# Adding up sixteen scan states with accumulating transfers, and moving upper adjacency products from a middle pass into the scan

## The chip, the cores and the metric

The kernel runs on one core of one Trainium2 chip. The metric is the device time of one launch in microseconds (us), as the median of several runs.

## What is computed

Two layers over a graph of N = 8192 nodes with 128 features, each with a residual. Layer 0 is a graph convolution with a symmetrically normalised adjacency matrix. Layer 1 is a graph convolution with the plain matrix, a layer norm and a selective state-space block (Mamba) that scans over the 8192 nodes with 256 inner channels and 16 states:

```
h = relu(layernorm(x));  D = sum(adj, axis=1);  d = D ** -0.5
x = x + relu(((adj * d[:, None] * d[None, :]) @ h) @ W.T + b)
h = relu(layernorm(x))
g = layernorm(relu(adj @ h @ gcn_w + gcn_b)) * ln_g + ln_b
xz = g @ w_in;  u = silu(conv4(xz[:, :256]));  z = xz[:, 256:]
dt, B, C = from u @ w_xp;  dt = softplus(dt @ w_dt + b_dt);  A = -exp(A_log)
s[t] = exp(dt[t] * A) * s[t-1] + dt[t] * B[t] * u[t]        # 256 x 16 states
y[t] = sum over the 16 states of s[t] * C[t]
x = x + ((y + u * D_skip) * silu(z)) @ w_out
```

All arithmetic is float32. The matrix is 256 MB, does not fit on the core, and is read more than once.

## The kernel before

**Tiling.** The output nodes are cut into 8 strips of 1024 columns. A block is 256 source nodes by one strip: 1 MB in SBUF, two pieces of 128 x 1024. A product here is one 128x128 by 128x512 matrix product; a block needs 4 of them for each layer. A float32 product shows as two PE records, a product of split operands (float32r) as one.

**Pass A** reads the whole matrix, adds up the degrees on VectorE (line 550), and forms layer 0 for every block on or below the diagonal (line 731).

**The middle (pass B)** goes through the strips from 6 down to 0 and reads the blocks above the diagonal once more. For layer 0 they complete the strip; a strip of layer 0 then gives 1024 nodes of layer 1's input `h1`, which are just the source nodes that the next strips need. So layer 1's upper products are formed from the same loads. Strip 6 (`firsts`) does this in plain float32, 16 products for each layer. Strips 5 to 0 split every operand in a high and a low float32r part: ScalarE writes the high parts (`high_part`, lines 1021 and 1024), VectorE subtracts for the low parts (`low_part`, lines 572 and 577), and TensorE forms high x high, high x low and low x high (`split_product`, line 813). That is 6 matmuls per piece and layer. `adj_parts` has two buffers, so ScalarE may start piece r only when TensorE has finished piece r-2. VectorE also completes the strip before (`complete`, seven stages, one after each of the first seven pieces), and ScalarE normalises it after piece 7 (`layer1_input`). Strips 5, 4, 3, 2, 1, 0 have 16, 24, 32, 40, 48, 56 pieces.

**The scan stage (pass C)** runs over 16 chunks of 512 nodes. A chunk has 16 slots, one for each state; slot g of the whole stage is state g mod 16 of chunk g div 16. In slot g VectorE multiplies (line 653) and scans twice (line 664, once for each half of the channels); GpSimd multiplies the state by C (line 458); ScalarE forms the next decay (line 1099). TensorE broadcasts row B for the next slot (line 874), which it may do only when the scans of slot g-1 are done, because the PSUM banks are shared. The other steps of a chunk stand in fixed slots: `chunk_at(g, STAGE)` says in which. Counted within a chunk, the convolution and gate products (lines 928, 932) are in slots 4 to 7, line 940 in 10, `dt` in 12 and 13, `gcn` in 13, the output products (line 909) in 9, skip, gate and residual on VectorE in 4, 5 and 9. TensorE works ahead on the strips of layer 1 that lie after it: `products[g]` spreads the products of strips 1 to 7 evenly over slots -19 to 204, at the end of each slot (line 853). Strip 7 is whole before slot 205. Slots -19 to -1 have no scan yet.

**The sum over the states.** GpSimd adds the two states of a pair (line 462), in all but the last 3 chunks, and TensorE adds the pairs up in PSUM, by products with the identity (line 890): two for each added pair, four for each pair that was not added. The ring of state buffers, `hs`, has 8 entries; an entry comes free when its identity products are done:

```
                    if g >= HSB:

                        dve.wait_ge(nsum_done, (g - HSB) // 2 + 1)
```

Layer 1's upper sums of strips 0 to 6 go to DRAM in the middle (`move_layer1`) and come back in the scan stage, where VectorE adds them (line 640).

**Queues.** SP issues all loads of the matrix (line 393) and, in the scan stage, the rows of C (line 418), in slot order; a load of C waits for GpSimd's products two pairs back. ScalarE issues the small transfers. GpSimd issues none.

## Time and profile before

| | |
|---|---|
| median of 3 runs | 2683.72 us (2681.23 to 2686.16) |
| the profiled execution, its own time | 2687.66 us |
| its span | 2685.8 us, so 1.9 us lie around it |
| mean granted TensorE clock | 0.954 of full speed |
| busy in the span | PE 87%, DVE 78%, ACT 36%, POOL 35% |
| HBM traffic | 239 GB/s over the span |

The stages follow each other: pass A to 792 us, the middle to 1427 us, the slots before the first scan to 1508.65 us, the scan to the end. In the profile a row gives an engine, a line, an operation, output <- inputs, and the mean time of one in ns; "idle before" is how long the engine had nothing to do and who ended that. PE durations contain the pipeline's tail, so the spacing of matmuls in a dense run, not their duration, is what one costs.

### The profile page before, as it was taken

Reading aid. Unit: us, or ns where it says so; the run is one execution under the profiler, and the core shown is the slowest. Engines: PE = TensorE matmul, PEld = TensorE weight load, DVE = VectorE, ACT = ScalarE, POOL = GpSimd, SP = SyncE. Lnnn points to the kernel's source line nnn. Section 1 sums busy time; section 2 is a strip of 40 time slices with the busy share of each in tenths; the row PEclk is TensorE's granted clock in tenths of the full one; section 3 lists DMA queues with packets and bytes.
Section 4 is the critical chain, followed back from the end, with each engine's and each line's share of the span. In section 5 each row is a group of like instructions: output and inputs, shape, how many; then the busy total and the mean of one; then the engine's idle time right before and its main releaser. Section 6 shows DMA issues by size and latency. Waiting matters only on the chain.

```text
span 2685.8 us, 22298 instructions
## 1 busy us (share of the span) xinstructions
PE 2325.4 (87%) x7072; PEld 1314.6 (49%) x7072; DVE 2082.0 (78%) x2079; ACT 979.5 (36%) x1696; POOL 936.9 (35%) x409
## 2 busy tenths in 40 slices
PE   0347688999999999999999989999999989997776
PEld 0113344444447888888885444444444444443333
DVE  5888888886645666566652599999999899999997
ACT  0000000000004555555552455555545555555552
POOL 0000000000000000000000388777778788787554
PEclk9978789999999999999999999999999999998898
DMA  8999999898766555555547655555555555551121
GB/s 337 380 398 412 394 393 388 356 404 321 263 247 236 214 214 216 197 213 196 199 183 266 231 198 210 207 208 204 198 211 213 197 207 206 204 196 63 67 75 52
DMA packets 108325, 643.02 MB, mean 239 GB/s; under 512 B 14225, under 2 KB 15025, under 8 KB 42673
## 3 DMA queue, kind: packets, MB, share of 16 engines
q1 hardware_dynamic: 92160, 604.02, 59.3%
q10 hardware_dynamic: 16048, 37.57, 4.0%
q8 instruction: 58, 0.95, 0.1%
q14 instruction: 59, 0.48, 0.0%
HBM read 625.28 MB, written 16.25 MB: 239 GB/s over the span
## 4 chain that ended last, share of the span: by engine, by line
PE 57%; DVE 28%; issue 8%; ACT 3%; ACTq 1%; DMA 1%; DVEq 0%; POOL 0%; SPq 0%; POOLq 0%
PE ps L813 21%; PE ps L731 13%; DVE arena L550 11%; PE ps L853 10%; DVE arena L664 6%; DVE ps L653 6%; PE ps L890 4%; PE ps L928 4%; PE ps L753 2%; ACTq L958 1%; DMA diag_h<-adj 1%; PE ps L874 1%; PE ps L909 1%; DVE ring L664 1%; PE ps L932 1%
## 5 line engine op out<-in xcount | busy, mean ns | idle before, releaser
L813 PE MATMUL ps<-adj_parts,h_parts 128*128 128x512 f32 x2592 | 593.7, 391 | 2.5 <-ACT adj_parts L1024 2.2
L442 POOL TENSOR_TENSOR rstd<-base,minus_half 128x8 f32<-128x8 f32 (+1 forms) x40 | 84.7, 2118 | 1450.7 <-DVE base L490 877.9
L853 PE MATMUL ps<-ring,diag_h 128*128 128x512 f32 x1152 | 549.0, 611 | 0.3 <-DVE arena L640 0.2
L458 POOL TENSOR_TENSOR arena<-arena 128x1024 f32<-128x1024 f32 x192 | 458.5, 2394 | 251.1 <-ACT state L1091 251.1
L813 PEld LDWEIGHTS ps<-adj_parts,h_parts 128*128 128x128 f32 x2592 | 485.0, 188 | 108.6 <-ACT adj_parts L1024 4.7
L550 DVE TENSOR_TENSOR arena<-arena,ring 128x2048 f32<-128x2048 f32 x208 | 476.8, 2292 | 67.0 <-DMA ring<-adj 49.2
L731 PE MATMUL ps<-ring,arena 128*128 128x512 f32 x928 | 437.7, 633 | 62.4 <-DMA ring<-adj 62.4
L664 DVE TENSOR_TENSOR_SCAN arena<-arena,state,ps 128x512 f32<-128x512 f32 x384 | 470.6, 1267 | 26.1 <-DVE ps L653 1.0
L853 PEld LDWEIGHTS ps<-ring,diag_h 128*128 128x128 f32 x1152 | 223.8, 196 | 252.4 <-issue 249.3
L1099 ACT ACTIVATE arena<-arena,a_sb 128x512 f32<-128x512 f32 x512 | 338.3, 708 | 0.4
L577 DVE TENSOR_TENSOR adj_parts<-ring,adj_parts 128x1024 fp32r<-128x1024 f32 x216 | 264.0, 1224 | 94.3 <-ACT adj_parts L1024 83.5
L731 PEld LDWEIGHTS ps<-ring,arena 128*128 128x128 f32 x928 | 187.4, 204 | 305.5 <-issue 305.5
L653 DVE TENSOR_TENSOR ps<-arena,ps 128x1024 f32<-128x1024 f32 x256 | 311.3, 1216 | 22.1 <-PE ps L874 21.1
L874 PE MATMUL ps<-parts,pick 96*128 96x512 f32 x256 | 181.2, 708 | 101.2 <-DVE arena L664 87.8
L1024 ACT ACTIVATE adj_parts<-ring 128x1024 fp32r<-128x1024 f32 x216 | 226.7, 1052 | 112.9 <-PE ps L813 110.9
L965 ACT ACTIVATE arena<-arena,nmr,rstd 128x128 f32<-128x128 f32 x128 | 51.9, 482 | 497.4 <-DVE nmr L494 497.4
L890 PE MATMUL ps<-arena,ident 128*128 128x512 f32 x456 | 229.9, 637 | 0.0
L462 POOL TENSOR_TENSOR arena<-arena 128x1024 f32<-128x1024 f32 x78 | 183.7, 2356 | 6.1
L664 DVE TENSOR_TENSOR_SCAN ring<-arena,state,ps 128x512 f32<-128x512 f32 x128 | 156.9, 1267 | 24.9 <-ACT arena L1099 18.1
L753 PE MATMUL ps<-ones,arena 128*128 128x1 f32 x256 | 47.2, 319 | 142.1 <-DVE arena L550 142.1
L458 POOL TENSOR_TENSOR ring<-ring,arena 128x1024 f32<-128x1024 f32 x64 | 151.3, 2365 | 24.5 <-ACT state L1091 24.5
L874 PEld LDWEIGHTS ps<-parts,pick 96*128 96x128 f32 x256 | 50.1, 196 | 203.7 <-issue 203.7
(85 smaller groups left out, 1783.1 us busy)
## 6 DMA issues: line engine op xcount, KB each, us to landing
ring<-adj SPq DMA_DIRECT2D x480, 1024.0 KB, 6.5
arena<-c_scratch SPq DMA_DIRECT2D x128, 512.0 KB, 3.8
diag_h<-adj SPq DMA_DIRECT2D x32, 1024.0 KB, 12.2
arena<-x ACTq DMA_DIRECT2D x16, 512.0 KB, 4.7
x_scratch<-arena ACTq DMA_DIRECT2D x8, 512.0 KB, 3.0
arena<-x_scratch ACTq DMA_DIRECT2D x16, 256.0 KB, 4.3
out<-arena ACTq DMA_DIRECT2D x16, 256.0 KB, 3.0
lower_scratch<-arena ACTq DMA_DIRECT2D x7, 512.0 KB, 2.6
```

The costliest lines, as they stand in the source:

```text
L458: nc.gpsimd.tensor_tensor(buf, buf, c_row, ALU.mult).then_inc(mult_done, 1)
L550: nc.vector.tensor_tensor(rowacc, rowacc, v, ALU.add).then_inc(adds_done, 1)
L577: nc.vector.tensor_tensor(adj_parts[:, buf, 1, :], ring[:, slot_of[q], a * STRIP:(a + 1) * STRIP], adj_parts[:, buf, 0, :].bitcast(F32), A ...
L653: nc.vector.tensor_tensor(dbu_ps[g % 2], w[k % 2], b_ps[g % 2].unsqueeze(1).to_broadcast([P, HALVES, T]), ALU.mult)\
L664: nc.vector.tensor_tensor_scan(hs[g % HSB][:, h, :], da[g % 2][:, h, :], dbu_ps[g % 2][:, h, :], state[:, h, n:n + 1], ALU.mult, ALU.add). ...
L731: last = nc.tensor.matmul(acc[:, c, :], tile_of(h, JT * s + a), blk[:, a * STRIP + c * MM:a * STRIP + (c + 1) * MM], start=start and a == ...
L813: last = nc.tensor.matmul(acc[:, c, :], h_parts[:, blk % 2, layer, h_part, a * F:(a + 1) * F], adj_parts[:, buf, adj_part, c * MM:(c + 1) ...
L853: last = nc.tensor.matmul((acc_c if i else y_ps)[:, c, :], tile_of(h1, JT * s + a), blk[:, a * STRIP + c * MM:a * STRIP + (c + 1) * MM], s ...
L874: nc.tensor.matmul(b_ps[(g + 1) % 2], pick[:, nn:nn + 1].to_broadcast([KP, P]), pv[0:KP, :], start=True, stop=True).then_inc(b_ready, 1)
L890: last = nc.tensor.matmul(y_ps[:, h, :], ident[:, :], term[:, h, :], start=pair == 0 and j == 0, stop=pair == DS // 2 - 1 and j == len(ter ...
L1024: nc.scalar.activation(adj_parts[:, buf, 0, :], ring[:, slot_of[q], a * STRIP:(a + 1) * STRIP], ACT.Copy).then_inc(hi_ready, 1)
L1099: last = nc.scalar.activation(da[(g + 1) % 2][:, h, :], dt[k % 2][:, h, :], ACT.Exp, scale=a_sb[:, h, n:n + 1])
```

## The change

Two things. First, the sum over the states. GpSimd writes its products of states 0 and 1 into a new tile `y_pair`; the product pairs of states 2 to 13 are added to it by six transfers from SBUF to SBUF of 128 x 2048 floats (1 MB) each with `accum_op=ALU.add`, issued from GpSimd's queue. Each waits until the one before has landed (`y_added`). TensorE then takes the two halves of `y_pair` in slot 16 (slot 0 of the next chunk, four identity products), and the last pair, states 14 and 15, directly in slot 18 (four more). GpSimd's own additions are gone. `hs` has 6 entries in place of 8; entries of states 2 to 13 come free when their transfer has landed.

Second, strips 2 to 6 form layer 1's upper products in the scan stage, in plain float32, and no longer in the middle; their blocks are read again there, and their upper sums no longer go through DRAM. Strips 0 and 1 keep the old way.

```diff
-HSB = 8
+HSB = 6
+DEFERRED = 2
-NSUM = 6
+YSUM, LAST_PAIR = 16, 18
-SPARED = 3
...
-    rows_of = {i: list(range(BPS * (i + 1))) for i in range(NS)}
+    rows_of = {i: list(range(BPS * (i + 1) if i < DEFERRED else NB)) for i in range(NS)}
...
+        PAIRS = DS // 2
+
+        def added(G):
+
+            k, p = divmod(G, PAIRS)
+            return 16 * ((PAIRS - 2) * k + min(max(p - 1, 0), PAIRS - 2))
...
-                    nc.gpsimd.tensor_tensor(buf, buf, c_row, ALU.mult).then_inc(mult_done, 1)
-                    if g % 2 and g // 2 < PAIRS_ADDED:
+                    k, n = divmod(g, DS)
+                    if n == 0 and k:
+
+                        pool.wait_ge(nsum_done, 2 * k - 1)
+                    nc.gpsimd.tensor_tensor(y_sums[n] if n < 2 else buf, buf, c_row, ALU.mult)\
+                        .then_inc(mult_done, 1)
+                    if n % 2 and 2 < n < DS - 2:
+
                         pool.wait_ge(mult_done, g + 1)
-                        even = hs[(g - 1) % HSB]
-                        nc.gpsimd.tensor_tensor(even, even, buf, ALU.add).then_inc(pair_done, 1)
+                        pool.wait_ge(y_added, added(g // 2))
+                        pool.dma_start(y_pair, hs_pairs[g // 2 % (HSB // 2)], accum_op=ALU.add)\
+                            .then_inc(y_added, 16)
...
-                        dve.wait_ge(nsum_done, (g - HSB) // 2 + 1)
+                        k_old, n_old = divmod(g - HSB, DS)
+                        if n_old < 2:
+                            dve.wait_ge(mult_done, g - HSB + 1)
+                        elif n_old < DS - 2:
+                            dve.wait_ge(y_added, added((g - HSB) // 2 + 1))
+                        else:
+                            dve.wait_ge(nsum_done, 2 * (k_old + 1))
...
-            for layer, acc, h in ((0, acc0[NS % 2], h0), (1, acc1, h1)):
...
+            for s in firsts:
+                product(acc0[NS % 2], h0, s, arrived(load_at["B", NS - 2, s]), s == firsts[0], s == firsts[-1])\
+                    .then_inc(blocks_done, 1)
...
                     last = split_product(acc0[i % 2], r, a, 0, start, stop)
-                    if stop:
-                        last.then_inc(layer0_sum, 1)
-                    if start:
-
-                        pe.wait_ge(l1_staged, n)
-                    split_product(acc1, r, a, 1, start, stop).then_inc(pieces_done, 1)
+                    if i < DEFERRED:
+                        if stop:
+                            last.then_inc(layer0_sum, 1)
+                        if start and i < DEFERRED - 1:
+
+                            pe.wait_ge(l1_staged, DEFERRED - 1 - i)
+                        last = split_product(acc1, r, a, 1, start, stop)
+                    last.then_inc(pieces_done, 1)
...
+                k = chunk_at(g, YSUM)
+                if k is not None:
+                    pe.wait_ge(mult_done, DS * k + 2)
+                    pe.wait_ge(y_added, added(PAIRS * (k + 1) - 1))
+                    if k:
+                        pe.wait_ge(y_free, k)
+                    for j in range(2):
                         for h in range(HALVES):
-                            last = nc.tensor.matmul(y_ps[:, h, :], ident[:, :], term[:, h, :],
-                                                    start=pair == 0 and j == 0,
-                                                    stop=pair == DS // 2 - 1 and j == len(terms) - 1)
+                            last = nc.tensor.matmul(y_ps[:, h, :], ident[:, :], y_sums[j][:, h, :],
+                                                    start=j == 0, stop=False)
+                    last.then_inc(nsum_done, 1)
+                k = chunk_at(g, LAST_PAIR)
+                if k is not None:
+                    pe.wait_ge(mult_done, DS * (k + 1))
...
```

`high_part` and `low_part` also make the parts of `h1` only for strips 0 and 1.

How the instructions stand. TensorE from the first products of the middle to its last, before (line 731 is `firsts`, 788 the product with layer 0's weights, 813 the split products):

```order
L731 MATMUL ps<-ring,arena 128x512 x16
L731 MATMUL ps<-ring,diag_h 128x512 x16
L813 MATMUL ps<-adj_parts,h_parts 128x512 x12
L788 MATMUL ps<-w0t_sb,arena 128x128 x8
L813 MATMUL ps<-adj_parts,h_parts 128x512 x192
L788 MATMUL ps<-w0t_sb,arena 128x128 x8
L813 MATMUL ps<-adj_parts,h_parts 128x512 x288
L788 MATMUL ps<-w0t_sb,arena 128x128 x8
L813 MATMUL ps<-adj_parts,h_parts 128x512 x384
L788 MATMUL ps<-w0t_sb,arena 128x128 x8
L813 MATMUL ps<-adj_parts,h_parts 128x512 x480
```

and the same place now (lines 759, 816 and 835):

```order
L759 MATMUL ps<-ring,arena 128x512 x16
L835 MATMUL ps<-adj_parts,h_parts 128x512 x6
L816 MATMUL ps<-w0t_sb,arena 128x128 x8
L835 MATMUL ps<-adj_parts,h_parts 128x512 x96
L816 MATMUL ps<-w0t_sb,arena 128x128 x8
L835 MATMUL ps<-adj_parts,h_parts 128x512 x144
L816 MATMUL ps<-w0t_sb,arena 128x128 x8
L835 MATMUL ps<-adj_parts,h_parts 128x512 x192
L816 MATMUL ps<-w0t_sb,arena 128x128 x8
L835 MATMUL ps<-adj_parts,h_parts 128x512 x246
```

The 16 plain products of layer 1 are gone, and a piece of strips 5 to 2 has 6 matmuls where it had 12.

TensorE in slots 4 to 8 of a chunk in the scan stage, before (line 874 opens a slot; 890 is an identity product, 928 and 932 the convolution and gate, 853 the products of the strips ahead):

```order
L874 MATMUL ps<-parts,pick 128x512
L890 MATMUL ps<-ring,ident 128x512 x2
L928 MATMUL ps<-arena,w_conv 128x512 x4
L853 MATMUL ps<-ring,diag_h 128x512 x3
L874 MATMUL ps<-parts,pick 128x512
L928 MATMUL ps<-arena,w_conv 128x512 x4
L853 MATMUL ps<-ring,diag_h 128x512 x2
L874 MATMUL ps<-parts,pick 128x512
L890 MATMUL ps<-arena,ident 128x512 x2
L932 MATMUL ps<-arena,w_in_sb 128x512
L853 MATMUL ps<-ring,diag_h 128x512 x2
```

and slots 0 to 4 of a chunk now (898 opens a slot; 908 is the sum that the transfers made, 916 the last pair, 943 the transpose, 954 the convolution, 877 the products ahead):

```order
L898 MATMUL ps<-parts,pick 128x512
L908 MATMUL ps<-arena,ident 128x512 x4
L877 MATMUL ps<-ring,diag_h 128x512 x3
L898 MATMUL ps<-parts,pick 128x512
L877 MATMUL ps<-ring,diag_h 128x512 x4
L898 MATMUL ps<-parts,pick 128x512
L916 MATMUL ps<-arena,ident 128x512 x4
L877 MATMUL ps<-ring,diag_h 128x512 x3
L898 MATMUL ps<-parts,pick 128x512
L943 MATMUL ps<-ident,arena 128x128 x4
L877 MATMUL ps<-ring,diag_h 128x512 x4
```

Every other slot had two identity products; now slots 0 and 2 have four each and the others none. A slot ends with 3 or 4 products of a strip ahead where it had 2 or 3.

GpSimd in the scan stage, before (458 multiplies by C, 462 adds a pair):

```order
L458 TENSOR_TENSOR arena<-arena 128x1024 [waits c_in0,state_saved] x2
L462 TENSOR_TENSOR arena<-arena 128x1024 [waits mult_done]
L458 TENSOR_TENSOR arena<-arena 128x1024 [waits c_in1,state_saved] x2
L462 TENSOR_TENSOR arena<-arena 128x1024 [waits mult_done]
L458 TENSOR_TENSOR arena<-arena 128x1024 [waits c_in0,state_saved] x2
```

and now, from the first state of a chunk on (472 multiplies, 478 issues an accumulating transfer):

```order
L472 TENSOR_TENSOR arena<-arena 128x1024 [waits nsum_done,c_in0,state_saved]
L472 TENSOR_TENSOR arena<-arena 128x1024 [waits c_in0,state_saved]
L472 TENSOR_TENSOR ring<-ring,arena 128x1024 [waits c_in1,state_saved] x2
L478 DMA arena<-ring 128x2048 [waits y_added,mult_done]
L472 TENSOR_TENSOR arena<-arena 128x1024 [waits c_in0,state_saved] x2
L478 DMA arena<-arena 128x2048 [waits y_added,mult_done]
```

The addition of each pair is now a transfer, behind a wait for the transfer before it.

## Rows read from the trace of the kernel before

**Rows 1.** Windows by stage: stretch, us, busy us by engine, PEclk, DMA share, GB/s

```profile
105.00:450.00 345.00, 246.24 (x565) 119.33 (x566) 297.35 (x208) 16.84 (x36) 21.00 (x8) 0.84 0.95 389
...
820.00:1136.00 316.00, 314.29 (x1408) 258.45 (x1407) 203.63 (x310) 167.88 (x259) 7.00 (x4) 1.00 0.59 215
...
1454.00:1508.00 54.00, 51.76 (x137) 23.89 (x135) 8.38 (x25) 15.44 (x22) 2.01 (x2) 1.00 0.65 231
1508.65:2448.00 939.35, 865.96 (x2282) 411.80 (x2280) 857.90 (x826) 494.32 (x898) 744.89 (x318) 0.97 0.57 203
2448.00:2686.00 238.00, 164.65 (x400) 77.29 (x399) 212.52 (x197) 107.63 (x200) 133.53 (x57) 0.88 0.18 63
```

**Rows 2.** Chain that ended last, pieces: start us, us, what, in the middle

```profile
1050.03 89.20 PE ps L813 x392
```

**Rows 3.** Timeline of the middle's start, all engines: layer 1's sixteen products

```profile
806.32 13.90 PE L731 MATMUL ps<-ring,diag_h 128*128 128x512 f32 x32
```

**Rows 4.** Timeline of one block in the middle, ScalarE and VectorE

```profile
1163.85 0.42 ACT L1021 ACTIVATE h_parts<-arena 128x256 fp32r<-128x256 f32 x1 [2.51 <-PE ps L813]
1164.18 0.40 ACT L1021 ACTIVATE h_parts<-diag_h 128x256 fp32r<-128x256 f32 x1
1164.48 1.04 ACT L1024 ACTIVATE adj_parts<-ring 128x1024 fp32r<-128x1024 f32 x1
...
1165.56 1.23 DVE L577 TENSOR_TENSOR adj_parts<-ring,adj_parts 128x1024 fp32r<-128x1024 f32 x1
```

**Rows 5.** Costliest groups and the rest of them, by line

```profile
L813 PE MATMUL ps<-adj_parts,h_parts 128*128 128x512 f32 x2592 | 593.7, 391 | 2.5 <-ACT adj_parts L1024 2.2
L588 DVE TENSOR_TENSOR arena<-ps,arena 128x1024 f32<-128x1024 f32 x7 | 8.5, 1218 | 1.7 <-PE ps L813 1.7
L890 PE MATMUL ps<-arena,ident 128*128 128x512 f32 x456 | 229.9, 637 | 0.0
L890 PE MATMUL ps<-ring,ident 128*128 128x512 f32 x152 | 73.4, 613 | 0.0
```

**Rows 6.** Timeline of a strip's start in the middle, completion of the strip before

```profile
1289.08 3.18 ACT L965 ACTIVATE diag_h<-arena,nmr,rstd 128x128 f32<-128x128 f32 x8
```

**Rows 7.** Chain that ended last, first float32 products of the scan stage

```profile
1427.10 27.48 PE ps L853 x64
```

**Rows 8.** Timeline of one chunk in the scan stage, VectorE

```profile
1903.29 2.45 DVE L664 TENSOR_TENSOR_SCAN ring<-arena,state,ps 128x512 f32<-128x512 f32 x2
1905.66 1.21 DVE L653 TENSOR_TENSOR ps<-arena,ps 128x1024 f32<-128x1024 f32 x1
1906.99 2.45 DVE L664 TENSOR_TENSOR_SCAN ring<-arena,state,ps 128x512 f32<-128x512 f32 x2
```

**Rows 9.** Waits of TensorE on VectorE at line 949

```profile
DVE arena L673: 36.7, 15
```

**Rows 10.** Timeline of GpSimd in the scan stage: a product, a pair's addition

```profile
1903.95 2.36 POOL L458 TENSOR_TENSOR arena<-arena 128x1024 f32<-128x1024 f32 x1 [3.02 <-ACT state L1091]
1906.39 2.35 POOL L462 TENSOR_TENSOR arena<-arena 128x1024 f32<-128x1024 f32 x1
```

**Rows 11.** DMA issues with median us to landing: pass A, middle, scan stage (two)

```profile
ring<-adj SPq DMA_DIRECT2D x214, 1024.0 KB, 8.7
...
ring<-adj SPq DMA_DIRECT2D x106, 1024.0 KB, 4.8
...
ring<-adj SPq DMA_DIRECT2D x113, 1024.0 KB, 5.6
arena<-c_scratch SPq DMA_DIRECT2D x96, 512.0 KB, 4.2
```

**Rows 12.** Timeline of the end, VectorE

```profile
2666.81 2.46 DVE L664 TENSOR_TENSOR_SCAN ring<-arena,state,ps 128x512 f32<-128x512 f32 x2
2676.23 1.41 DVE L705 SCALAR_TENSOR_TENSOR arena<-arena,cols_sb,ps 128x512 f32<-128x512 f32 x2 [6.97 <-PE ps L890]
```

More of the change, by code:

```diff
@@ L132, in build @@
     assert adds == NS * adds_per_strip
-    pieces_at = {}
-    pieces = 0
+    pieces_at, h_parts_at = {}, []
+    pieces = h_parts_made = 0
     for q, (phase, i, _) in enumerate(loads):
@@ L140, in build @@
             pieces_at[q] = pieces
+            h_parts_made += 2 if i < DEFERRED else 1
+            h_parts_at.append(h_parts_made)
         elif phase != "A":
@@ L236, in build @@
         da = [work2(HALVES, T) for _ in range(2)]
-        hs = [work2(HALVES, T) for _ in range(HSB - 2)]
-        hs += [ring[:, RING - 1, b * HALVES * T:(b + 1) * HALVES * T].rearrange("p (a b) -> p a b", a=HALVES)
-               for b in range(2)]
+        hs_pairs = [work2(2 * HALVES * T) for _ in range(HSB // 2 - 1)] + [ring[:, RING - 1, :]]
+        hs = [hs_pairs[b // 2][:, b % 2 * HALVES * T:(b % 2 + 1) * HALVES * T].rearrange("p (a b) -> p a b", a=HALVES)
+              for b in range(HSB)]
+        y_pair = work2(2 * HALVES * T)
+        y_sums = [y_pair[:, b * HALVES * T:(b + 1) * HALVES * T].rearrange("p (a b) -> p a b", a=HALVES)
+                  for b in range(2)]
         csb = [work2(2, T) for _ in range(2)]
@@ L336, in build @@
         mult_done = sem("mult_done")
-        pair_done = sem("pair_done")
+        y_added = sem("y_added")
         nsum_done = sem("nsum_done")
@@ L568, in low_part @@
                 if a == 0:
-                    s = loads[q][2]
-                    dve.wait_ge(h_hi_ready, 2 * (blk + 1))
-                    for layer, h in enumerate((h0, h1)):
+                    _, i, s = loads[q]
+                    dve.wait_ge(h_hi_ready, h_parts_at[blk])
+                    for layer, h in enumerate((h0, h1) if i < DEFERRED else (h0,)):
                         nc.vector.tensor_tensor(h_parts[:, blk % 2, layer, 1, :],
@@ L875, in _ @@
                                      start=True, stop=True).then_inc(b_ready, 1)
[L876 to L892 removed]
+                k = chunk_at(g, YSUM)
[5 more added lines that the diff above has]
+                    for j in range(2):
+                        for h in range(HALVES):
+                            last = nc.tensor.matmul(y_ps[:, h, :], ident[:, :], y_sums[j][:, h, :],
[4 more added lines that the diff above has]
+                    pe.wait_ge(mult_done, DS * (k + 1))
+                    for j in range(2):
+                        for h in range(HALVES):
+                            last = nc.tensor.matmul(y_ps[:, h, :], ident[:, :],
+                                                    hs[(DS * k + DS - 2 + j) % HSB][:, h, :],
+                                                    start=False, stop=j == 1)
                     last.then_inc(nsum_done, 1)
@@ L1016, in high_part @@
                 if a == 0:
-                    s = loads[q][2]
-                    for layer, h in enumerate((h0, h1)):
+                    _, i, s = loads[q]
+                    for layer, h in enumerate((h0, h1) if i < DEFERRED else (h0,)):
                         if layer:
@@ L1064, in _ @@
                     r += 1
-                    if m == (1 if n == 1 else 0):
-                        move_layer1(n - 1, i + 1)
+                    if m == 0 and i + 1 < DEFERRED:
+                        move_layer1(i + 1)
                     if m == 7:
                         layer1_input(n)
-            move_layer1(NS - 2, 0)
+            move_layer1(0)
             layer1_input(NS - 1)
@@ L1101, in _ @@
                     last.then_inc(da_ready, 1)
-                for i in range(NS - 1):
+                for i in range(DEFERRED):
                     if max(handover[i] - 2, FIRST_SLOT) == g:
```

51 lines of the change are left out of this document (16 added, 35 removed).

## Prediction

> **What bounds the kernel now.** I read the windows by stage first, since the change touches two stages with different limits. In the middle, strips 5 to 2, TensorE is busy 314.29 of 316.00 us at the full granted clock, while VectorE has 203.63 and ScalarE 167.88 [rows 1]: TensorE bounds it. In the scan stage up to slot 205 VectorE is busy 857.90 of 939.35 us and TensorE 865.96, at 0.97 of the clock [rows 1]; which of the two sets the pace is read from the timeline. From one scan pair to the next VectorE takes 1906.99 - 1903.29 = 3.70 us without a gap [rows 8], so 16 slots are at least 59.2 us, and its once-a-chunk steps come on top. The stretch has 205 slots, 12.81 chunks, so a chunk takes 939.35 / 12.81 = 73.3 us. TensorE's spacing is dense where it works, but it waits at `dt` for VectorE, 36.7 us in 15 times, 2.4 us a chunk [rows 9]. So VectorE leads, with TensorE close behind. After slot 205 TensorE has slack (164.65 of 238.00 us [rows 1]).
>
> **What a matmul costs.** The mean of 391 ns for a split matmul [rows 5] holds the pipeline's tail; 392 of them took 89.20 us [rows 2], 0.2276 us each. A float32 product is two records; 64 took 27.48 us [rows 7], so 0.859 us a product. A moved product thus costs 3 x 0.2276 = 0.683 us in the middle and 0.859 us in the scan: the move pays only if the middle gets faster and the scan has room.
>
> **The middle: -102 us.** Layer 1's 16 products of strip 6 go: -13.9 us [rows 3]; the parts of the first piece were ready before they began. Strips 5 to 2 have 112 pieces. TensorE's need falls from 12 to 6 x 0.2276 = 1.37 us a piece, below VectorE's 1.23 + 0.34 / 2 for its subtractions only by a little, so the handover through two buffers becomes the limit. For the first buffer it is a ring: ScalarE's high part of `h0`, 1164.18 - 1163.85 = 0.33 us; the high part of the matrix, to VectorE's start 1165.56 - 1164.48 = 1.08 us; the subtraction 1.23 us [rows 4]; two matmuls, one spacing and one duration, 0.23 + 0.39 us; two handoffs, taken as the 0.05 us that lies between ScalarE's end and VectorE's start: 3.36 us for two pieces. 56 blocks x 3.36 = 188 us. Completing a strip puts on VectorE four operations of 1.22 us [rows 5] and some 2.7 us of statistics, and on ScalarE 3.18 us of normalising [rows 6]; 10.8 us in all, of which the ring's slack on VectorE (3.36 - 2.80 us a block, over four blocks) takes 2.2. So 4 x 8.6 = 34 us. Together 222 us where 316 were [rows 1]: -94 us. TensorE will idle a fifth of the time. In pass A, busy 246.24 of 345.00 us, it was granted 0.84, and after slot 205, busy 164.65 of 238.00, 0.88 [rows 1], which is a mix of 1.2 and 2.4 GHz. At 1.2 GHz a piece would take TensorE 2.73 us, 1.05 more than the ring. With a fifth of the time at that level some 16 pieces lose 17 us; with none, nothing. I take 6. Sum: -13.9 - 94 + 6 = -102 us, bounds -113 and -88. Strips 1 and 0 stay.
>
> **Before the first scan: +17 us.** Strips 2 to 6 bring 60 blocks, 240 products, so the evenly spread list grows from 544 to 784 over 224 slots. The 19 slots before the first scan get 66 where they had 46. TensorE is busy 51.76 of 54.00 us there [rows 1] and sets the time: 20 x 0.859 = +17 us. Nothing covers it.
>
> **The scan up to slot 205: +35 us.** Products in 16 slots rise from 38.9 to 56: +14.7 us. Identity products fall from 16 to 8: -6.9 us. The rest of TensorE's work in a chunk, counted in the order by the same spacings, is 17.7 us: before 33.4 + 13.7 + 17.7 = 64.8, now 48.1 + 6.9 + 17.7 = 72.7 us. The wait at `dt` is built in, because it is for the scan of its own slot; with 2.4 us for it TensorE needs 75.1 us, over VectorE's 73.3. So **TensorE becomes the bound by a hair**, and what it waits for now counts in full. New is the wait for the sixth transfer in slot 0. VectorE is freed from nothing, and nearly all of its work stays.
>
> The price of an accumulating transfer has no row: GpSimd issues none now. Call p the time from one's issue to the next one's. Below, a load of 1 MB lands in 4.8 us in the middle and 5.6 in the scan stage, and the issue comes on top [rows 11]: p = 6. Above, it has to read two operands, so two such loads one after the other, at the scan's level 11.2, and at pass A's crowded level 17.4 us [rows 11]. I take 8, nearer the single load, since source and target both lie in SBUF. The Trainium skill (DMA: Bandwidth & Descriptors, on the anatomy of a DMA from GpSimd) gives 2.0 us plus the bytes at 436 GB/s; by that estimate it would be 4.4 us and the wait nothing. The last transfer is issued about 2.8 us after the scans of state 13 (ScalarE's save, then 2.36 us of product [rows 10]) and TensorE reaches the sum two slots, 7.4 us, after them: with p = 8 it waits about 3 us. Two thirds of that lie in slot 15's long work on VectorE. I count 1 us: 76.1 us a chunk, (76.1 - 73.3) x 12.81 = +36, say +35 us; bounds 73.6 us (clock back at 1.00, slack used well) and, by the transfers, rival one.
>
> GpSimd falls from 24 x 2.36 = 56.6 us of a chunk to 37.8 and six issues, so it can wait. Its queue holds the products behind a transfer's wait, and SP's loads of C and of the matrix stand behind those products; the ring of six blocks gives the matrix some 30 us, C's rows two pairs. Fewer additions there also disturb VectorE less; I count nothing, since TensorE leads.
>
> **After slot 205: 0 us.** From the last scan's end to the skip 2676.23 - 2669.27 = 7.0 us pass [rows 12], in identity products held back; now a product, 2.4 us, and four identity products, 3.4 us, plus handoffs. No difference that counts.
>
> **The sum** is -102 + 17 + 35 = -50 us: 2687.66 - 50 = 2638 us for an execution like the profiled one. That lay 3.9 us over the median of 2683.72, so I forecast **2634 us**. Its own range, with the bounds of each term, is 2604 to 2665.
>
> **Rival one: the transfers set the pace, slower (32%).** They are chained. From the last of a chunk to the first of the next lie six slots and the statistics, 6 x 3.70 + 4.4 = 26.6 us, then five times p: a chunk takes 26.6 + 5p. Break-even is where the scan gives back 85 us, at 79.9 us a chunk, p = 10.7. At p = 11.5 (two loads at the scan's level, and the issue) it is 84.1 us: +138 us in place of +35, 2634 + 103 = 2737 us. For it speaks the space on the DMA engines: share 0.57 of 73.3 us is 41.8 us; 4.25 more blocks a chunk at pass A's 389 GB/s for 0.95 of the engines add 10.9, and six transfers 15.4 if each byte costs once, 30.7 if twice: 68 or 83 us, against 76. Against it: source and target in SBUF, and the loads of the matrix are far ahead. The Trainium skill (Collectives: The Full Stack, on where bytes move and the add happens) says that a reducing transfer reads two sources and so moves half as much as a copy. By that rule the 83 us hold, and the DMA engines bound the chunk: 2634 + (83 - 76.1) x 12.81 = 2722 us. No row here shows such a transfer.
>
> **Rival two: the middle gives less (8%).** If the clock falls further than I took, so that a third of the blocks run at 1.2 GHz (2 x 2.73 us) and the rest in 3.36, or if the handoffs that TensorE hid cost as much, a block takes 4.1 us on the mean, strips 5 to 2 take 230 + 34 = 264 us, and 42 us of the gain are lost: 2676 us, within or just under the bound of what can be told.
>
> **Rival three: TensorE isn't the bound after all (10%).** The transfers land early, the clock is 1.00, a chunk stays at 73.6 us, and the scan costs 4 in place of 35: 2603 us. The forecast itself has 50%.
>
> **Chances.** About 0.2% (5 us) can be told from no change. Faster: 50 + 10, less 2 for the forecast's tail and plus 3 from rival two = 0.61; same 0.07; slower 0.32. The range takes in rival three and, above, the doubled transfer: 2600 to 2745; outside lie transfers at the crowded level, p = 17.4, over 3000 us.
>
> **What would show it.** Right: windows in which strips 5 to 2 take 215 to 235 us with TensorE's share near 0.8; 17 us more before the first scan; chunks of 75 to 77 us with TensorE busy over 95%, and scans that wait for line 898; the transfers landing within 8 us. Wrong: VectorE's scans or GpSimd waiting for `y_pair`'s transfers, landing times over 10 us, a DMA share near 1, or chunks over 80 us.

## The result, and the profile after

The changed kernel takes **2888.08 us** (median of 4 runs, 2886.75 to 2892.76), the kernel before beside it 2683.03 us: ratio 1.0764, 95% interval 1.0747 to 1.0782. That is 7.6% slower; forecast were 2634 us, in a range up to 2745.

The profiled execution has a span of 2886.0 us and a time of its own of 2887.79; the kernel before had a span of 2685.8. The windows below answer to those in [rows 1]: the first lies in strips 5 to 2 of the middle and is read by its shares, the next two are the scan stage up to slot 205 and what follows.

Windows of the kernel after; us, then busy time by engine, granted clock, DMA share, GB/s:

```profile
792.00:1032.00 240.00, 211.01 (x763) 133.97 (x761) 188.35 (x276) 153.38 (x212) 8.63 (x5) 0.96 0.81 293
1421.50:2634.90 1213.40, 992.26 (x2517) 471.25 (x2515) 858.93 (x827) 494.76 (x897) 558.08 (x292) 0.89 0.86 268
2634.90:2886.00 251.10, 108.41 (x255) 53.26 (x254) 211.80 (x197) 106.59 (x197) 144.96 (x74) 0.69 0.61 144
```

| stretch | before, us | after, us | difference | forecast |
|---|---|---|---|---|
| up to the last product with layer 0's weights (line 788, now 816) | 1425.05 | 1320.22 | -104.8 | -102 |
| from there to the first scan's product | 83.6 | 101.3 | +17.7 | +17 |
| scan stage up to slot 205 | 939.4 | 1213.4 | +274.0 | +35 |
| after slot 205 | 237.7 | 251.1 | +13.4 | 0 |
| sum | 2685.8 | 2886.0 | +200.2 | -50 |

The first two rows are good to some us only: the kernels below that share the changed kernel's code up to the first scan reach it between 1419.2 and 1428.0 us, those that share the code of the kernel before between 1501.9 and 1508.65. Between the means of the two groups lie 81 us, where 85 were forecast.

So the middle gave about what was forecast, and the scan stage took back more than twice that: a chunk, the stretch over 12.81, went from 73.3 to **94.7 us**. VectorE's busy time there is the same as before (858.93 us, 857.90 in [rows 1]), so all of the 274 us are time in which VectorE waited. TensorE's busy time rose to 992.26 us at a clock of 0.89, and it fills 82% of the stretch: it isn't the bound either. The chain that ended last, over the whole span, and the landings point at what is:

```profile
PE 40%; DMA 28%; DVE 17%; issue 6%; POOL 4%; ACT 4%; ACTq 1%; DVEq 0%; POOLq 0%; SPq 0%
...
ring<-adj SPq DMA_DIRECT2D x540, 1024.0 KB, 7.4
arena<-c_scratch SPq DMA_DIRECT2D x128, 512.0 KB, 6.9
arena<-arena POOLq DMA_DIRECT2D x64, 1024.0 KB, 11.7
...
arena<-ring POOLq DMA_DIRECT2D x32, 1024.0 KB, 11.9
```

DMA holds 28% of that chain, where it had 1% in the kernel before. The 96 accumulating transfers (`arena<-arena` and `arena<-ring`, 16 chunks of six) land 11.7 and 11.9 us after their issue (medians).

Waits of the kernel after; total us, times, longest:

```profile
POOL arena L478 <- DMA arena<-arena: 237.6, 43, 9.7
DVE ps L675 <- PE ps L898: 199.2, 51, 13.4
...
POOL arena L478 <- DMA arena<-ring: 122.2, 21, 8.2
POOL arena L472 <- PE ps L908: 120.1, 15, 10.6
...
DVE arena L692 <- DMA arena<-arena: 71.8, 20, 5.1
```

GpSimd waits 360 us at line 478 for the transfer before. VectorE's products (line 675) wait 199.2 us for TensorE's line 898, and its scans (line 692) for the transfer that reads their buffer, of which there are now six in place of eight. Of the 96 issues 64 waited for the transfer before. How these waits hang together is seen in one chunk. GpSimd's issues, from its timeline:

```profile
1918.41 0.93 POOL L478 DMA_DIRECT2D arena<-ring  x1 [0.30 <-POOL ring L472]
...
1931.60 0.88 POOL L478 DMA_DIRECT2D arena<-arena  x1 [0.30 <-POOL arena L472]
...
1944.90 0.88 POOL L478 DMA_DIRECT2D arena<-arena  x1 [5.44 <-DMA arena<-arena]
...
1958.71 0.88 POOL L478 DMA_DIRECT2D arena<-ring  x1 [8.23 <-DMA arena<-arena]
...
1971.33 0.88 POOL L478 DMA_DIRECT2D arena<-arena  x1 [7.06 <-DMA arena<-ring]
...
1982.26 0.88 POOL L478 DMA_DIRECT2D arena<-arena  x1 [5.36 <-DMA arena<-arena]
...
2016.22 0.92 POOL L478 DMA_DIRECT2D arena<-arena  x1 [0.30 <-POOL arena L472]
```

TensorE and VectorE after the sixth issue, from their timelines:

```profile
1991.18 5.60 PE L908 MATMUL ps<-arena,ident 128*128 128x512 f32 x8 [13.41 <-DMA arena<-arena]
```

```profile
2002.20 1.23 DVE L675 TENSOR_TENSOR ps<-arena,ps 128x1024 f32<-128x1024 f32 x1 [13.36 <-PE ps L898]
```

Five spacings take 1982.26 - 1918.41 = 63.9 us, 12.8 each: that is the prediction's p, the time from one issue to the next. Four of the five ended with a landing; the first ended with GpSimd's own product. TensorE stands 13.41 us in slot 16 (line 908) for the sixth transfer, and its product for the next scan (line 898) is queued behind that wait, so VectorE stands 13.36 us too. From the sixth issue to the next chunk's first pass 2016.22 - 1982.26 = 34.0 us. With 63.9 that is this chunk's 97.8 us. It is rival one's loop with both of its terms larger.

Room on the DMA engines is not what holds this stretch of the loop up: from the last landing to VectorE's start, 1991.20 to 2002.20 us, their share is 0.09. They stand nearly idle while TensorE works off what was queued behind its wait.

### The profile page after: what moved, and what is told of

It reads as the page before. It is cut to its first block, busy times and chain, and to the rows that moved or that the text cites. A ratio compares the mean times of both kernels' runs of the same rounds, so it can differ in the third digit from the quotient of the medians.

```text
span 2886.0 us, 21222 instructions
## 1 busy us (share of the span) xinstructions
PE 2275.1 (79%) x6496; PEld 1216.8 (42%) x6496; DVE 2060.0 (71%) x2023; ACT 958.4 (33%) x1635; POOL 761.6 (26%) x401
## 3 DMA queue, kind: packets, MB, share of 16 engines
q0 software_dynamic: 13824, 100.67, 17.2%
## 4 chain that ended last, share of the span: by engine, by line
PE 40%; DMA 28%; DVE 17%; issue 6%; POOL 4%; ACT 4%; ACTq 1%; DVEq 0%; POOLq 0%; SPq 0%
DMA arena<-arena 18%; DVE arena L567 11%; PE ps L835 11%; PE ps L759 11%; DMA arena<-ring 9%; PE ps L877 8%; PE ps L908 3%; PE ps L954 3%; POOL arena L472 2%; DVE adj_parts L594 2%; ACT adj_parts L1050 2%; PE ps L781 2%; PE ps L916 1%; ACTq L984 1%; POOL ring L472 1%
## 5 line engine op out<-in xcount | busy, mean ns | idle before, releaser
L877 PE MATMUL ps<-ring,diag_h 128*128 128x512 f32 x1632 | 762.6, 610 | 2.6 <-DVE arena L662 1.4
L835 PE MATMUL ps<-adj_parts,h_parts 128*128 128x512 f32 x1920 | 479.1, 403 | 28.6 <-ACT adj_parts L1050 10.4
L692 DVE TENSOR_TENSOR_SCAN arena<-arena,state,ps 128x512 f32<-128x512 f32 x344 | 421.7, 1267 | 101.6 <-DMA arena<-arena 71.8
L472 POOL TENSOR_TENSOR arena<-arena 128x1024 f32<-128x1024 f32 x172 | 417.8, 2489 | 251.3 <-ACT state L1114 170.5
L877 PEld LDWEIGHTS ps<-ring,diag_h 128*128 128x128 f32 x1632 | 318.6, 197 | 373.5 <-issue 368.5
L675 DVE TENSOR_TENSOR ps<-arena,ps 128x1024 f32<-128x1024 f32 x256 | 311.6, 1217 | 200.1 <-PE ps L898 199.2
L835 PEld LDWEIGHTS ps<-adj_parts,h_parts 128*128 128x128 f32 x1920 | 355.8, 191 | 149.3 <-ACT adj_parts L1050 33.5
L692 DVE TENSOR_TENSOR_SCAN ring<-arena,state,ps 128x512 f32<-128x512 f32 x168 | 205.9, 1267 | 50.9 <-DMA arena<-ring 41.3
L908 PE MATMUL ps<-arena,ident 128*128 128x512 f32 x128 | 90.0, 868 | 187.9 <-issue 77.9
L472 POOL TENSOR_TENSOR ring<-ring,arena 128x1024 f32<-128x1024 f32 x74 | 182.2, 2523 | 85.0 <-ACT state L1114 84.8
L908 PEld LDWEIGHTS ps<-arena,ident 128*128 128x128 f32 x128 | 35.3, 291 | 237.5 <-issue 182.1
## 6 DMA issues: line engine op xcount, KB each, us to landing
arena<-arena POOLq DMA_DIRECT2D x64, 1024.0 KB, 11.7
arena<-ring POOLq DMA_DIRECT2D x32, 1024.0 KB, 11.9
```

The costliest lines, as they stand in the source:

```text
L472: nc.gpsimd.tensor_tensor(y_sums[n] if n < 2 else buf, buf, c_row, ALU.mult)\
L675: nc.vector.tensor_tensor(dbu_ps[g % 2], w[k % 2], b_ps[g % 2].unsqueeze(1).to_broadcast([P, HALVES, T]), ALU.mult)\
L692: nc.vector.tensor_tensor_scan(hs[g % HSB][:, h, :], da[g % 2][:, h, :], dbu_ps[g % 2][:, h, :], state[:, h, n:n + 1], ALU.mult, ALU.add). ...
L835: last = nc.tensor.matmul(acc[:, c, :], h_parts[:, blk % 2, layer, h_part, a * F:(a + 1) * F], adj_parts[:, buf, adj_part, c * MM:(c + 1) ...
L877: last = nc.tensor.matmul((acc_c if i else y_ps)[:, c, :], tile_of(h1, JT * s + a), blk[:, a * STRIP + c * MM:a * STRIP + (c + 1) * MM], s ...
L908: last = nc.tensor.matmul(y_ps[:, h, :], ident[:, :], y_sums[j][:, h, :], start=j == 0, stop=False)
```

## The experiments

A chunk is always the stretch from the first scan's product to the copy of slot 205, over 12.81. All times are medians, with ratios to the kernel before in the same series (2682.6 to 2683.9 us).

**The two halves of the change.** sums_only puts the transfers and the new way of summing into the kernel before and moves nothing; move_only moves the products (`DEFERRED = 2`) and keeps the sums of before; move_456 moves strips 4 to 6 alone, keeps the sums of before and spreads the products ahead anew from strip to strip.

```
-                        nc.gpsimd.tensor_tensor(even, even, buf, ALU.add).then_inc(pair_done, 1)
+                        pool.dma_start(y_pair, hs_pairs[g // 2 % (HSB // 2)], accum_op=ALU.add)\
+                            .then_inc(y_added, 16)
```

> The kernel before with the accumulating transfers alone; strips 0 to 6 form layer 1's upper products in the middle as before. Theory A, the chain of transfers sets the pace: each still has to land before the next is issued, so even without the added matrix loads a chunk takes 26.6 + 5p; with p between the 9.2 us that the changed kernel shows after slot 205 and its 13.3 before, 73 to 93 us, middle 82, so the scan to slot 205 costs 110 us more and the rest 13: about 2800 us. Theory B, only the added loads of the matrix crowd the transfers out: p falls to 9, a chunk stays at 73 us, 2690 us or less.

> The kernel before with the moved products alone; the states are added by GpSimd and by 16 identity products a chunk as before. The middle gains 105 us and the slots before the first scan cost 17.6, as in the changed kernel. TensorE then needs 64.8 + 14.7 + 2.4 = 81.9 us a chunk and bounds the scan: 8.6 x 12.8 = 110 us more, total about 2706 us. If the theory is wrong that TensorE's products of a chunk simply add up, and the added loads of 1 MB alone slow the scan, it comes out over 2760 us.

> The kernel before with only strips 4, 5 and 6 moved (24 blocks) and the old sums by GpSimd and identity products; the products ahead are spread anew from strip to strip. The middle gains 13.9 + about 28 us, the slots before the first scan cost 7, and TensorE needs 73 us a chunk, level with VectorE's 73.3, so 1 us a chunk more: about 2661 us. If two engines at the same load cost each other more (3 us a chunk), no change against before.

Measured: sums_only 2857.13 us (1.0644, 1.0627 to 1.0661), a chunk 85.7 us. move_only 2695.32 us (1.0048, 1.0032 to 1.0064), a chunk 80.96 us. move_456 2686.59 us (1.001, 1.0001 to 1.0019), a chunk 76.3 us.

The transfers alone cost 174 us, without a single moved product: more than theory A's 2800 us and 82 us a chunk, and theory B is out. The move alone is within 0.5%, at 81.0 us a chunk where 81.9 were expected: what the middle gives goes into the scan stage, where TensorE is now the bound, as its window from the first scan on shows:

```profile
1427.00:2464.00 1037.00, 1021.62 (x2725) 489.76 (x2723) 860.27 (x826) 491.81 (x898) 747.77 (x319) 1.00 0.65 237
```

1021.62 of 1037 us busy. That is what the change's sums were to relieve. move_456 missed its 2661 us by 26: its scan costs 3.0 us a chunk more than before in place of 1, as its text gave for two engines at the same load that cost each other more. With the transfers in place the move adds 31 us (2857 to 2888): the middle gives its part, but a chunk goes from 85.7 to 94.7 us, with more loads beside the transfers.

**What the transfers' price is made of.** plain_copy takes `accum_op` away and nothing else; the sum over the states is left out of the result by that. half_size lets GpSimd add the two states of a pair first, so each transfer has 512 KB. after_late lets TensorE read the sums two slots and the last pair one slot later. two_sums has two pairs of sum tiles, fed in turn by five transfers a chunk (12 identity products), and one matrix block less in the ring; two_sums_late has the later reading as well.

```
-                        pool.dma_start(y_pair, hs_pairs[g // 2 % (HSB // 2)], accum_op=ALU.add)\
+                        pool.dma_start(y_pair, hs_pairs[g // 2 % (HSB // 2)])\
```

```
-YSUM, LAST_PAIR = 16, 18
+YSUM, LAST_PAIR = 18, 19
```

> The changed kernel with the six transfers as plain copies of the same 1 MB from SBUF to SBUF, from the same queue and with the same waits; the sum over the states is left out (the last copied pair stands in its place). Theory A, reading a second operand makes the transfer long: the engines' time for one falls from 5.1 us to about 2.6, it lands in 6 to 8 us, and a chunk is bounded by TensorE at 76 to 78 us: 2640 to 2680 us. Theory B, GpSimd's queue and the crowd on the engines make it long: landing stays at 11 us or more and the time over 2820 us.

> The changed kernel with GpSimd adding the two states of a pair first, so that six transfers of 512 KB in place of 1 MB add them to a tile of half the size; TensorE takes 6 identity products a chunk in place of 8. If the loop through the sum tile sets the pace and a transfer costs a fixed part plus its bytes, p falls from 13 to 7 or 8: 6 x 7.5 + 1.7 + 14.2 (four products and two additions) + 3 = 64 us, so TensorE bounds with 71.0 + 2.4 us and a chunk takes 74 to 78 us: 2610 to 2670 us. If the fixed part is most of it, p stays over 10 us, a chunk at 80 or more, over 2700 us.

> The changed kernel with TensorE's sum of the transferred pairs in slot 18 in place of 16 and the last pair in 19 in place of 18. Theory A, a closed loop through the one sum tile sets the pace (six transfers one after the other, TensorE's reading of the tile, GpSimd's four products, the first transfer again: 6 x 13 + 3.4 + 9.4 + 3 = 94 us): where TensorE waits does not matter, a chunk stays at 93 to 95 us and the time at 2870 to 2900. Theory B, TensorE's wait in slot 16, with the row for slot 18 queued behind it, is a loss of its own: VectorE's 191 us of waits for that row go, and the time falls under 2750 us.

> The changed kernel with two sum tiles, so that a transfer waits for the one two before it, and with five transfers a chunk (pairs 0 and 1 are written by GpSimd); TensorE takes 12 identity products in place of 8, and the matrix's ring in the scan has 5 blocks in place of 6. Theory A, the wait for the landing of the one before (latency in a chain) sets the pace: TensorE bounds again with 72.7 + 3.4 + 2.4 = 78.5 us a chunk, about 2690 us. Theory B, the engines' capacity sets it: two transfers in flight land later each, 15 us and more, and the time stays over 2800 us.

> Two sum tiles and five transfers a chunk as in two_sums, but TensorE reads the sums two slots later (slots 18 and 19 of the chunk, as in after_late). Theory A: in two_sums the loop went over TensorE's wait for the last transfer, which stands ahead of the next products for the scans; the transfers of the next chunk begin some five slots after it, so 22.9 us of scans and statistics, a product and five transfers of 13 us made 94 us. Two slots of room take 7 us or more from it, and the second tile now relieves the first of the two: a chunk of 80 to 87 us, 2700 to 2790 us in all, below after_late's 2798.67. Theory B: the crowded DMA engines, not the waits' places, set the pace of 94 us: 2850 us or more.

Measured (p is the mean spacing of the issues in one chunk between 1915 and 2045 us, the gap runs from a chunk's last issue to the next first):

| kernel | us | ratio, interval | chunk, us | p, us | gap, us |
|---|---|---|---|---|---|
| the change | 2888.08 | 1.0764, 1.0747 to 1.0782 | 94.7 | 12.8 | 34.0 |
| sums_only | 2857.13 | 1.0644, 1.0627 to 1.0661 | 85.7 | 11.3 | 32.4 |
| plain_copy | 2745.73 | 1.0226, 1.0209 to 1.0243 | 84.8 | 10.9 | 29.0 |
| half_size | 2756.81 | 1.0284, 1.0251 to 1.0316 | 84.3 | 10.5 | 30.4 |
| after_late | 2798.67 | 1.0426, 1.0408 to 1.0443 | 87.4 | 13.4 | 22.9 |
| two_sums | 2891.59 | 1.0783, 1.0763 to 1.0802 | 94.2 | 10.4 | 53.7 |
| two_sums_late | 2816.48 | 1.0496, 1.0477 to 1.0514 | 88.6 | 11.4 | 45.6 |

Five p and the gap give each six-transfer kernel's chunk within 4 us. (two_sums has four spacings, and its gap is a pair of states longer.) p has a floor that is not the transfer's: an issue follows each pair of states, an eighth of a chunk, which is 9.6 us at the 76.8 us a chunk of quads_tail below; the gap's share by the same pace is three eighths, 28.8 us. Of the 21 us that the change's chunk above lies over 76.8, the spacings thus hold 16 and the gap 5, by estimate. half_size's p is only 0.9 us over the floor.

Two things enter: how long a transfer takes, and where its last landing is waited for. plain_copy and after_late came out between their theories, so each took away a part of the cause; half_size and two_sums came out on the slow side of theirs. Here are the transfers' queues in plain_copy, 1640 to 2400 us:

```profile
q0 software_dynamic: 7610, 55.40, 17.5%
...
arena<-arena POOLq DMA_DIRECT2D x35, 1024.0 KB, 9.5
```

and in the changed kernel, the same stretch, where the DMA share is 0.86 as against 0.79:

```profile
q0 software_dynamic: 6823, 49.61, 32.0%
...
arena<-arena POOLq DMA_DIRECT2D x32, 1024.0 KB, 12.0
```

A transfer is 144 packets (13824 over 96 for the whole kernel). So 6823 packets are 47.4 transfers at 0.320 x 760 / 47.4 = 5.13 us of all 16 engines each; in plain_copy 52.8 at 2.52 us. The second operand doubles the time on the engines, but of 12.0 us to landing it is 2.5. The Trainium skill (Collectives: The Full Stack, the bandwidth ceiling, on why ReduceScatter is half of AllGather) says of collectives that the reducing transfer reads two sources where a copy reads one, and so comes to about half the bandwidth. These rows agree for the add within SBUF: 5.13 against 2.52 us for the same megabyte. Most of the 12.0 us is not the transfer's own time on the engines: at the kernel's end, from 2640 us on with few other loads, a transfer still lands 8.2 us after its issue, and plain_copy's 6.6 us.

```profile
arena<-arena POOLq DMA_DIRECT2D x13, 1024.0 KB, 8.2
```

Reading the sums later took 11 us from the gap, since TensorE's wait then overlaps two more scans, and 89 us from the total; VectorE's wait for line 898 fell from 199.2 to 71.9 us. The second pair of tiles took GpSimd's waits for the transfer before away (its issues wait 0.30 us for their own product) and gained nothing. TensorE's one wait for the last landing remained, now with twice the identity products behind it, and C's rows arrive 11.5 us after their issue instead of 7.7, so GpSimd waits for those. As this kernel also has a block less and other counts, it shows that a second tile isn't enough, not what it is worth by itself. two_sums_late missed its theory A: 88.6 us a chunk for 80 to 87, 2816 us for 2700 to 2790, and it is slower than after_late, not faster.

**The same sums without transfers.** quads_move moves strips 2 to 6 as the change does, but GpSimd adds pairs and then pairs of pairs, so TensorE has the same 8 identity products a chunk; the eight buffers of before are back. quads_tail mends its end, where it waited for four states at once. quads_only is this with nothing moved, quads_tail_3456 with strip 2 left in the middle.

```
                         nc.gpsimd.tensor_tensor(even, even, buf, ALU.add).then_inc(pair_done, 1)
+                        if g % 4 == 3:
+                            pool.wait_ge(pair_done, 3 * (g // 4) + 2)
+                            first = hs[(g - 3) % HSB]
+                            nc.gpsimd.tensor_tensor(first, first, even, ALU.add).then_inc(pair_done, 1)
```

> The changed kernel's move of strips 2 to 6, with the sums made without transfers: GpSimd adds pairs and then pairs of pairs (28 operations of 2.36 us, 66 us a chunk), and TensorE takes 8 identity products a chunk, as many as with the transfers. It isolates what the transfers cost: if everything else was forecast right, a chunk takes TensorE's 72.7 + 2.4 us and up to 1 more, so the total is the forecast, 2625 to 2650 us. If GpSimd, busy 66 of 76 us and in bursts, holds the state buffers too long, VectorE waits for identity products and it comes out over 2680 us.

> quads_move, but in the last three chunks, where GpSimd adds nothing, TensorE takes each state as soon as its product is there and frees its buffer, instead of four at once. After slot 205 quads_move took 265 us where the kernel before took 238, with VectorE waiting 34.1 us for TensorE's identity products. Theory A: that wait is those 27 us; it goes, and the total is 2645 to 2655 us. Theory B: what is lost there is another wait (GpSimd and ScalarE), and the total stays at 2668 to 2675 us.

> The kernel before with GpSimd adding pairs and pairs of pairs, so that TensorE has 8 identity products a chunk and no transfer is issued; nothing is moved out of the middle, and the sums of the last three chunks go to TensorE state by state. Theory A (VectorE sets the pace of the scan stage before the change, TensorE's relief is worth nothing without the move): a chunk stays at 73 to 74 us, total 2675 to 2695 us. Theory B (TensorE's identity products cost time in the kernel before too): a chunk of 71 us or less, total below 2665 us. Theory C: GpSimd, now 24 times 2.36 us and 4 more additions a chunk, holds up the scans: over 2700 us.

> quads_tail with strips 3 to 6 moved instead of 2 to 6. Theory A (TensorE is the bound of the scan by a little once 56 products stand in 16 slots, and each strip moved costs there what it gains in the middle): the middle gives 20 to 25 us less and the scan 15 to 25 us back, total within 10 us of quads_tail. Theory B (VectorE bounds the scan already): only the middle's gain is lost, total 15 to 25 us over quads_tail.

| kernel | us | ratio, interval | first scan's product at | chunk, us | after slot 205, us |
|---|---|---|---|---|---|
| quads_move | 2674.30 | 0.9959, 0.9944 to 0.9974 | 1419.6 | 76.8 | 265.0 |
| quads_tail | 2640.05 | 0.9836, 0.9819 to 0.9853 | 1428.0 | 76.8 | 229.1 |
| quads_only | 2648.48 | 0.9873, 0.9857 to 0.9890 | 1503.6 | 71.1 | 232.9 |
| quads_tail_3456 | 2640.19 | 0.9838, 0.9823 to 0.9853 | 1444.6 | 74.9 | 231.8 |

quads_move came out 24 us over its forecast, all of it after slot 205, where it took 265.0 us; quads_tail shows that the end was to be had, and by 5 us more than its theory A gave. quads_tail beats both kernels, and it stands 6 us from the forecast of the change: 76.8 us a chunk where 76.1 were forecast. Its window over 760 us of the scan stage:

```profile
1640.00:2400.00 760.00, 725.03 (x1953) 346.73 (x1953) 664.58 (x647) 379.15 (x688) 676.93 (x287) 1.00 0.69 249
```

TensorE is busy 95% at the full clock, VectorE 87%. So moving and relieving TensorE together give the forecast's time, and what separates 2640 from 2888 us is how the states are summed, with the buffers, six for eight, that go with it. quads_only met its theory B, and that is a finding about the kernel before: with 6.9 us of identity products less in a chunk, and nothing else for VectorE, a chunk falls from 73.3 to 71.1 us. VectorE didn't hold the pace there alone. It also shows where the gain lies: 35 of the 44 us come from the relief with nothing moved, and all of the move adds 8. Against sums_only, which has the same 8 identity products and moves nothing either, it is 209 us faster. Moving strip 2 costs in the scan what it gives in the middle (theory A of quads_tail_3456).

**Room on the engines, or waiting?** Three last kernels on quads_tail. quads_ring5 has one matrix block less in the ring, as control; idle_accum adds six accumulating transfers of 1 MB a chunk, whose data nobody uses and for which only GpSimd waits, ahead of the next; idle_copy does the same with plain copies.

```
+                    if n in (1, 4, 6, 9, 12, 14):
+                        pool.wait_ge(idle_done, 16 * m)
+                        pool.dma_start(ring[:, RING - 2, :], h1[:, 0:BLOCK], accum_op=ALU.add)\
+                            .then_inc(idle_done, 16)
```

> quads_tail with the ring of matrix blocks in the scan stage at five instead of six: the control for the two kernels beside it, which need the block's room. Both theories: the loads land in 5.4 us and five blocks last over 30 us, so nothing changes, 2635 to 2650 us, a chunk of 76 to 78 us.

> quads_ring5 with six accumulating transfers of 1 MB a chunk on GpSimd's queue, spread over states 1, 4, 6, 9, 12 and 14, whose data nobody uses and for which nobody waits but GpSimd ahead of the next one; the result does not rest on them. Theory A (the change lost its time to the space on the DMA engines): their share was 0.69 of 76.8 us, 53 us a chunk, and six times 5.1 us come on top, 84 us a chunk, so the matrix and C arrive late, chunks of 82 to 86 us and a total over 2700 us. Theory B (it lost it to the waits for the transfers' landing, and engines with their share near 0.9 still deliver in time): chunks of 77 to 80 us, total 2645 to 2685 us.

> idle_accum with plain copies instead of accumulating transfers: 2.5 us of the engines each, 68 us a chunk with the rest. By both theories near quads_ring5, within 15 us of it. If idle_accum is much slower and this is not, the second operand's space on the engines is what costs; if both are slower alike, it is GpSimd's issuing or its waits for the landing.

Measured: quads_ring5 2639.49 us (0.984, 0.9824 to 0.9857), chunk 76.8; idle_accum 2705.72 us (1.0072, 1.0045 to 1.0099), chunk 81.9; idle_copy 2667.63 us (0.9947, 0.9932 to 0.9962), chunk 79.1. The same stretch of idle_accum, its window, two of its landings and one wait:

```profile
1640.00:2400.00 760.00, 699.66 (x1827) 332.18 (x1826) 651.21 (x602) 355.24 (x647) 676.95 (x323) 0.97 0.99 313
```

```profile
ring<-adj SPq DMA_DIRECT2D x130, 1024.0 KB, 11.2
ring<-diag_h POOLq DMA_DIRECT2D x55, 1024.0 KB, 11.9
```

```profile
POOL ring L482 <- DMA ring<-diag_h: 74.1, 27, 5.9
```

The DMA engines are full, at 0.99, and the matrix lands after 11.2 us (5.1 in quads_ring5). That traffic costs 66 us against the control (idle_accum's runs lie between 2692 and 2711 us, so 53 to 72); copies, with a share of 0.87, cost 28, more than the 15 expected. Theory A had said chunks of 82 to 86 us and over 2700 in all, B 77 to 80: chunk and total are A's, at its edge. Part of the 66 is GpSimd's waiting and issuing, which these kernels don't separate from the room. But the change stands 182 us higher still, with the same number and size of transfers, though its engines are less full (0.86 in its window above). By this subtraction the 182 us belong to what idle_accum lacks: scans that wait for buffers, of which there are six for eight, and products and scans that wait for the chain.

## Why the prediction was wrong

Against its own sum for the profiled execution, 2638 us, the profile has 2888: 250 us more. Term by term that is -3 in the middle, +1 before the first scan (both within the spread of some us told above), +239 in the scan up to slot 205, +13 after it.

- **The middle, -102: right, measured -104.8.** VectorE's subtractions there repeat every 3.45 us for a block, where the handover's ring was worked out at 3.36; TensorE is busy 88% at a granted 0.96.
- **Before the first scan, +17: right, measured +17.7.**
- **The scan, TensorE's part: right within 1 us a chunk.** Without transfers, 76.8 us in quads_tail against 76.1. That VectorE led in the kernel before, at 73.3 us, was only half right: quads_only runs at 71.1, and move_456 pays 3.0 us a chunk for products that should have fitted beside VectorE.
- **The scan, the transfers' part: this step failed.** The prediction took p = 8 "nearer the single load, since source and target both lie in SBUF", and counted 1 us a chunk of waiting. p is 12.8 in the changed kernel. Source and target in SBUF gave no cheap transfer: it lands in 8.2 us with few other loads and in 12.0 in the scan stage. The bounds 6 to 17.4 held it; the choice within them rested on nothing that was measured. It also priced the transfer as if its neighbours stayed as they were, though the moved loads bring the DMA share from 0.57 to 0.69 (quads_tail) and the transfers to 0.86. And 8 lies under the pace of the scans, a pair of states in 9.6 us at 76.8 a chunk: the slack was from there to the break-even of 10.7, about 1 us a transfer.
- **The loop, 26.6 + 5p: right in form, the constant too small.** It has to be 34.0: the last landing lies on it (8.9 us from the sixth issue to TensorE's start at 1991.18), then come 5.6 us of identity products, some 5 us of products for a strip ahead and the product for the scan, and only then, at 2002.20, VectorE goes on. With p = 8 the loop would have been about 74 us by estimate, under TensorE's 76; with 12.8 it is 97.8. Rival one named this mechanism, had 32%, and with both terms too low came out at 2737 us.
- **The price by room on the engines: right, and not decisive.** The prediction's 83 us, worked out for a transfer that costs each byte twice, was met by idle_accum's 81.9 at a share of 0.99. It is the smaller part: by subtraction 66 us of 248.
- **After slot 205, 0: wrong by 13 us.** The loop runs there too: TensorE waits 21.4 us in three times for landings at line 908, and its granted clock, 0.88 before, is 0.69. quads_tail takes 229.1 us for the stretch, less than before.

That quads_tail stands so near the forecast's 2634 us is in part luck: its scan up to slot 205 took 9 us more than was worked out, and the stretch after it 9 us less.

What stays open is how the 182 us divide among the buffers (six for eight), GpSimd's chain and TensorE's wait: no run has the change's transfers with eight buffers, none has sums without transfers with six, and the two-tile kernels changed too much at once.

## What to carry to other kernels

Before work is handed to a DMA in a loop, follow the loop to its end: the last landing, who reads it, and what is queued behind that reader on an in-order engine. Multiply an unmeasured price by its place in the chain, here five times and once more for the landing; if the break-even lies inside its bounds, the forecast is open, whatever the likeliest value. And try the adding on an engine with slack first: GpSimd had room for four more additions a chunk (it is busy 89% in quads_tail's window), and with them the same move and the same relief of TensorE took 1.6% off, where the transfers put 7.6% on.

## What was unexpected of the hardware

- An accumulating transfer of 1 MB within SBUF takes 5.13 us of all sixteen engines, a plain one 2.52. Yet in the change it lands 8.2 us after the issue with few other loads and 12.0 among them; plain_copy's 6.6 and 9.5.
- The idle plain copies of idle_copy land sooner than plain_copy's at about the same DMA share: 6.7 us in the scan stage, and 4.7 from 2440 us on. Why is not shown. The Trainium skill (DMA: Bandwidth & Descriptors, anatomy of a DMA from GpSimd) gives 2.0 us plus the bytes at 436 GB/s, 4.4 us by estimate: the 4.7 agree, the others lie well over it.
- Half the bytes don't land in half the time: 512 KB took 7.6 and 8.8 us in half_size's scan stage (DMA share 0.80), 1 MB 12.0 in the change's (0.86).
- The issue of an accumulating transfer is recorded with 0.88 us, of a plain one with 0.59, but GpSimd's next product can start 0.61 us after the issue's start in both (1944.90 to 1945.51 us in the change, 1985.87 to 1986.48 in plain_copy).
- Transfers for which no scan waits still cost 66 us; the matrix then lands in 11.2 us in place of 5.1.
